# Graph layers on one core: edge keys made earlier, two groups of them compared in the first product unit, and the third adjacency load put behind the first three loads of H rows

## What is computed

```
msgs = x[src]
out = x @ root + bias
for r in range(8):
    mask = (edge_type == r)
    sums = segment_sum(msgs * mask, dst)
    cnt  = segment_sum(mask, dst)
    out  = out + (sums / max(cnt, 1)) @ weight[r]
u = out
z = concat([u, x]) @ w_gate + b_gate
h = tanh(u) * z + x * (1 - z)
```

## Time and profile before

| What | us |
|---|---|
| runs of the kernel | 1172.08, 1175.61, 1187.93 |
| span of the profiled execution | 1185.5 |
| TensorE busy | 1102.5 (93%) |
| VectorE busy | 702.4 (59%) |
| ScalarE busy | 386.1 (33%) |
| GpSimd busy | 386.3 (33%) |
| end of the units on TensorE | 524.9 |
| first spread | 527.8 to 537.5 |
| second spread begins | 548.7 |

### The profile page before, as it was taken

One profiled execution on the slowest core, in us unless ns is written; L12 is line 12 of the kernel. 1 busy time (PEld: TensorE's weight loads), 2 busy tenths in 40 slices (PEclk: granted clock), 3 DMA queues, 4 the chain that ended last, 5 costly groups with the idle time before them and its releaser, 6 DMA issues.

```text
span 1185.5 us, 14272 instructions
## 1 busy us (share of the span) xinstructions
PE 1102.5 (93%) x5481; PEld 916.7 (77%) x5481; DVE 702.4 (59%) x1369; ACT 386.1 (33%) x598; POOL 386.3 (33%) x268
## 2 busy tenths in 40 slices
PE   5999999999999999986999998999979897989896
PEld 4778888888888888876999998887747675777774
DVE  7486666566666532105667766475587556656557
ACT  3222222222223332222332333441443324146652
POOL 6036655646565466623232230000100002410015
PEclk8999999999999999998999998999989898989997
DMA  8956678877567575457556442632330202576857
GB/s 324 416 184 143 143 208 202 204 221 160 143 142 147 129 169 125 75 155 225 173 168 207 114 119 74 209 142 77 55 85 38 71 2 73 192 233 231 271 171 248
DMA packets 84612, 191.77 MB, mean 162 GB/s; under 512 B 29080, under 2 KB 45275, under 8 KB 76089
## 3 DMA queue, kind: packets, MB, share of 16 engines
q1 hardware_dynamic: 36362, 123.40, 32.8%
q0 software_dynamic: 31968, 35.38, 14.1%
q10 hardware_dynamic: 16206, 32.00, 9.2%
HBM read 136.60 MB, written 54.15 MB: 161 GB/s over the span
## 4 chain that ended last, share of the span: by engine, by line
PE 70%; DMA 10%; DVE 10%; POOL 5%; issue 3%; ACT 2%; POOLq 0%; SPq 0%; DVEq 0%
PE ps L483 60%; POOL adj_scratch L1833 5%; DMA stage<-in_w_e 4%; DMA adj_scratch<-cnt,idx 3%; DVE rl L340 3%; PE ps L724 2%; PE ps L761 2%; DVE EQ L1236 1%; DMA stage<-h_scratch 1%; PE ps L690 1%; ACT rh L330 1%; PE ps L473 1%; PE ps L772 1%; PE ps L707 1%; DMA stage<-in_w_rel 1%
## 5 line engine op out<-in xcount | busy, mean ns | idle before, releaser
L340 DVE TENSOR_TENSOR rl<-stage,rh 128x512 fp32r<-128x512 f32 (+1 forms) x282 | 224.4, 826 | 336.4 <-ACT rh L330 316.5
L330 ACT CAST rh<-stage 128x512 fp32r<-128x512 f32 (+1 forms) x288 | 193.8, 709 | 530.9 <-PE ps L483 282.6
L1833 POOL DMA_INDIRECT adj_scratch<-cnt,idx x162 | 260.2, 1606 | 221.6 <-DMA adj_scratch<-cnt,idx 88.5
L483 PE MATMUL ps<-rh,xTh 128*125 128x512 f32 x800 | 316.5, 396 | 2.5 <-DVE U L1304 1.5
L483 PE MATMUL ps<-rl,xTh 128*125 128x512 f32 x800 | 315.0, 394 | 0.0
L483 PE MATMUL ps<-rh,xTl 128*125 128x512 f32 x800 | 314.6, 393 | 0.0
L483 PE MATMUL ps<-rh,Ar 125*125 125x342 f32 x600 | 193.3, 327 | 19.0 <-DVE rl L340 11.2
L483 PE MATMUL ps<-rl,Ar 125*125 125x342 f32 x600 | 192.3, 325 | 0.0
L483 PEld LDWEIGHTS ps<-rh,xTh 128*125 128x125 f32 x800 | 148.4, 185 | 40.3 <-DVE U L1304 2.0
L483 PEld LDWEIGHTS ps<-rh,xTl 128*125 128x125 f32 x800 | 148.7, 186 | 37.2
L483 PEld LDWEIGHTS ps<-rl,xTh 128*125 128x125 f32 x800 | 148.6, 186 | 36.0
(11 more groups left out here) (263 smaller groups left out, 1222.8 us busy)
## 6 DMA issues: line engine op xcount, KB each, us to landing
stage<-in_w_rel SPq DMA_DIRECT2D x32, 1024.0 KB
stage<-h_scratch SPq DMA_DIRECT2D x24, 855.0 KB
stage<-in_w_e SPq DMA_DIRECT2D x16, 1024.0 KB
adj_scratch<-Z POOLq DMA_DIRECT2D x16, 767.0 KB, 22.9
KR<-key_scratch ACTq DMA_DIRECT2D x27, 384.0 KB
h_scratch<-He ACTq DMA_DIRECT2D x40, 257.0 KB, 9.8
h_scratch<-He ACTq DMA_DIRECT2D x40, 256.0 KB, 9.1
stage<-in_w_gate SPq DMA_DIRECT2D x8, 1024.0 KB
```

The costliest lines, as they stand in the source:

```text
L330: e.copy(h, s).then_inc(*a_hi.up(*[("hi", t) for t in step(i)]))
L340: e.tensor_tensor(l, s, h.bitcast(F32), ALU.subtract).then_inc(*own.up(*[("lo", t) for t in step(i)]))
L483: ins = e.matmul(ps[0:P, b, 0:width], a, m, start=first and n == 0, stop=last and n == len(parts) - 1)
L1833: e.indirect_dma_start(accd, bass.IndirectOffsetOnAxis(ap=idx[:, n:n + 1], axis=0), cnt[:, n:n + 1], None, compute_op=ALU.add).then_inc(*d ...
```

## The change

Five edits:

1. DVE makes the keys directly behind the low parts of the first eight tiles, before chunk 2 of x is measured. ACT writes them to memory before the square root of chunk 2 (`root("n1", 2)`), and reads the first four groups back before it casts the turned chunk 3. TensorE transposes the keys behind chunk 0 and no longer behind chunk 1, and DVE copies them after chunk 3 is normalised, which is before chunk 3 is turned.
2. TensorE turns chunk c + 1, not c + 2, in the middle of chunk c, for c = 1 to 3: one chunk later than before.
3. DVE compares two groups of keys (EARLY = 2) in the first half of unit 0: group 0 before it evicts chunk 3, group 1 before chunk 4. All later groups move forward by two places, one half of a unit. ACT issues the rows of groups 4, 5 and 6 together at the first place.
4. SP loads the third adjacency (r = 2) behind the third load of H rows. The others keep their place behind the first load of their r.
5. The gate's bias (`BB`) is loaded late, behind the router's weights, and no longer at the start.

```diff
--- before.py
+++ after.py
@@ -39,6 +39,7 @@
 SW = 2048
 NHE = 8
 NB = 8
+EARLY = 2
 WINDOWS = (1, 5)
 ROWS = [[(slice(0, 128), c * P, 128)] for c in range(C - 1)] + [[(slice(0, 112), 500, 112), (slice(112, P), 612, 13)]]
 HALF = (slice(0, 512), slice(512, D))
@@ -405,7 +406,6 @@
             rows_in(U128, 4, d_x[4], ("x", 4))
             on.wait_ge(*at("x", 3))
             e.dma_start(BA128[:], rbias.partition_broadcast(128)).then_inc(*d_ba.up(("rbias",)))
-            e.dma_start(BB128[:], gbias.partition_broadcast(128)).then_inc(*d_bb.up(("gbias",)))
 
             def adjacency_in(r):
                 on.wait_ge(*at("adj", r - 2))
@@ -419,12 +419,13 @@
             for r in range(R):
                 for q in range(3):
                     load(first("h", r, q, 0))
-                    if q == 0 and 2 <= r + 2 < R:
+                    if q == (2 if r == 0 else 0) and 2 <= r + 2 < R:
                         adjacency_in(r + 2)
             for g in range(first("gate", 0, 0), first("gate", 0, 0) + 2):
                 load(g)
             e.dma_start(rw[:].rearrange("p k n -> p (k n)"), router).then_inc(*d_sm.up())
             e.dma_start(b1s[:].rearrange("p k n -> p (k n)"), b1).then_inc(*d_sm.up(("small",)))
+            e.dma_start(BB128[:], gbias.partition_broadcast(128)).then_inc(*d_bb.up(("gbias",)))
             for c in range(C):
                 on.wait_ge(*at("spread", R - 1, 2, C - 1))
                 rows_in(X128, c, d_xc[c], ("x again", c))
@@ -526,7 +527,7 @@
             turn("n1", 1, U, ("n1", "norm", 1))
 
             def keys_turned(c):
-                if c == 1:
+                if c == 0:
                     b, freed = banks.take(("keys",), ("key columns",))
                     for g in range(2):
                         on.wait_ge(*at("key rows"))
@@ -542,7 +543,7 @@
                     first = unit_tile(unit, hf, 0)
                     if unit == 0 and hf == 0:
                         by_chunk(("unit", 0, 0), first, 8, x_stat, freed, lambda c: (("n1", "lo", c, 1),), keys_turned,
-                                 lambda c: turn("n1", c + 2, U, ("n1", "norm", c + 2)) if c + 2 < C else None)
+                                 lambda c: turn("n1", c + 1, U, ("n1", "norm", c + 1)) if 1 <= c < C - 1 else None)
                         end_chunks(("unit", 0, 0))
                     else:
                         by_tile(("unit", unit, hf), first, 8, x_stat, freed)
@@ -970,24 +971,27 @@
             turned("n1", 0, xTh)
             turned("n1", 1, xTh)
             highs(8)
+            on.wait_ge(*at("key rows"))
+            e.dma_start(keyd.rearrange("(g p) q -> p g q", g=2), kr1[:]).then_inc(*d_key.up(("keys out",)))
             for c in range(2, C):
                 root("n1", c)
                 if c == 3:
-                    on.wait_ge(*at("key rows"))
-                    e.dma_start(keyd.rearrange("(g p) q -> p g q", g=2), kr1[:]).then_inc(*d_key.up(("keys out",)))
+                    for g in range(4):
+                        key_rows(g)
                 turned("n1", c, xTh)
             highs(10)
-            for g in range(4):
-                key_rows(g)
             g, s = 0, 0
             for unit in range(R + 1):
                 for hf in range(2):
                     if unit or hf:
                         for k in range(8):
                             highs(unit_tile(unit, hf, k) + RT)
-                            if k % 8 in WINDOWS and g < NG:
-                                if g + 4 < NG:
-                                    key_rows(g + 4)
+                            if k % 8 in WINDOWS and g < NG - EARLY:
+                                if g == 0:
+                                    for early in range(EARLY):
+                                        key_rows(4 + early)
+                                if g + EARLY + 4 < NG:
+                                    key_rows(g + EARLY + 4)
                                 g += 1
                     if unit == R and hf == 1:
                         adjacency_copy(0)
@@ -1255,6 +1259,12 @@
             lows(4)
             turned("n1", 1, xTh, xTl)
             lows(8)
+            on.wait_ge(*at("edges"))
+            e.scalar_tensor_tensor(out=kr0[:], in0=er[0][0:HR], scalar=float(RI), in1=er[1][0:HR], op0=ALU.mult, op1=ALU.add).then_inc(
+                *v_row.up(("key place",)))
+            on.wait_ge(*at("key place"))
+            e.scalar_tensor_tensor(out=kr1[:], in0=er[2][0:HR], scalar=float(N), in1=kr0[:], op0=ALU.mult, op1=ALU.add).then_inc(
+                *v_row.up(("key sum",)))
             measured(2)
             normed(2)
             for c in range(2, C):
@@ -1264,13 +1274,6 @@
                 if c + 1 < C:
                     normed(c + 1)
                 if c == 2:
-                    on.wait_ge(*at("edges"))
-                    e.scalar_tensor_tensor(out=kr0[:], in0=er[0][0:HR], scalar=float(RI), in1=er[1][0:HR], op0=ALU.mult, op1=ALU.add).then_inc(
-                        *v_row.up(("key place",)))
-                    on.wait_ge(*at("key place"))
-                    e.scalar_tensor_tensor(out=kr1[:], in0=er[2][0:HR], scalar=float(N), in1=kr0[:], op0=ALU.mult, op1=ALU.add).then_inc(
-                        *v_row.up(("key sum",)))
-                if c == 3:
                     on.wait_ge(*at("keys turned"))
                     e.tensor_copy(kc[:], ps[:, banks.of["keys",], 0:TILES]).then_inc(*v_out.up(("key columns",)))
                     on.wait_ge(*at("key columns"))
@@ -1297,6 +1300,9 @@
                                 g += 1
                     for c in range(C):
                         b = banks.of["unit", unit, hf, c]
+                        if unit == 0 and hf == 0 and c >= C - EARLY:
+                            key_window(g)
+                            g += 1
                         if unit == 0:
                             on.wait_ge(*at("unit", 0, hf, c))
                             on.wait_ge(*at("rbias"))
```

## The result

| | before | changed |
|---|---|---|
| median of 20 runs | 1182.18 | 1184.52 |
| lowest to highest | 1169.95 to 1194.42 | 1179.60 to 1190.13 |
| span of the profiled execution | 1185.5 | 1185.8 |

What follows compares the result with a forecast made beforehand. TensorE, busy 93% of the span, bounds the kernel, so only its waits can be won: 1185.5 - 16.5 (first spreads) + 9.2 (start) = 1178.2. Forecast 1179, own range 1175 to 1184, overall range 1166 to 1187.

Steps and rivals of the forecast that it cites:

- The stall: TensorE's waits at the first two spreads, 2.98 and 11.19 us, from late adjacency additions; removal with clock effects: 16.5 off.
- the release: TensorE's release by a VectorE eviction after the early comparisons, at 82.95 before; forecast 91.7 to 92.6.
- wait at tile 10: TensorE stands about 4.3 us for tile 10's low part, which VectorE makes behind two early comparisons.
- So 0 to 0.3 us of wait stay: At the second spread: H rows ready 7.0 to 7.9 us after the units' end, first spread ending at 7.96.
- The sum: For the first two spreads: 2.98 + 11.19 + 1.67 + 1 - 0.3 = 16.5 us off, bounds 15.5 and 17.5.
- The clock term: Second spread began slowly after its wait; full clock there to win 1 us, bounds 0 and 1.7.
- Nothing: Loading the gate's bias late, around 725 with the queue idle to 744, was to change no time.
- The median run has little left to win: Without the stall the profiled execution gives 1171.1, fastest run 1172.08; the start's 9.2 us are paid in every run.
- the four that change the time: Rivals: start costs less (0.2), runs differ for another reason (0.17), start costs more (0.07), additions become the bound (0.04).
- the start costs more: Rival: weight load at 9 us and slower restart make the start cost 13 to 16, total 1183 to 1187; chance 0.07.
- The additions become bound: Rival: additions land late again amid second-half weight traffic; at 18.5 us a group, 37 late, 1216; chance 0.04.
- The early comparisons do nothing for the additions: Rival: zeroes land only at 67, so earlier indices don't help; counted inside the forecast, no chance of its own.

Runs made afterwards that it cites:

- experiment 2: Kernel before, without the additions of the last two of 27 groups of keys; 1175.56 us, ratio 0.9863 to the kernel before.
- experiment 5: Changed kernel with EARLY = 0, all comparisons at their old places; 1177.36 us, ratio 1.0014 to the kernel before.
- experiment 6: Changed kernel with GpSimd's step on the key rows ahead of its 16 zeroing transfers; 1178.36 us, ratio 1.0041 to the kernel before.
- experiment 3: Changed kernel with GpSimd's copy of adjacency 0 held until the second spread's low parts are made; 1185.18 us, ratio 0.9955 to the kernel before.
- experiment 1: Kernel before with only the third adjacency load moved behind three H loads; 1181.55 us, ratio 0.9885 to the kernel before.
- experiment 4: Changed kernel with GpSimd's copy and first addition held behind the second and third spreads' low parts; 1180.49 us, ratio 0.9893 to the kernel before.
- experiment 7: Changed kernel with the third adjacency load back behind the first H load; 1185.46 us, ratio 1.0077 to the kernel before.
- experiment 8: Kernel before with the later adjacency load, both GpSimd holds and the first comparison in VectorE's idle time; 1172.23 us, ratio 0.9963 to the kernel before.
- experiment 12: Changed kernel with EARLY = 1, key rows ahead of the zeroing transfers and both GpSimd holds; 1173.32 us, ratio 0.9874 to the kernel before.
- experiment 13: Changed kernel with the gate's bias loaded at the start again; 1180.82 us, ratio 1.0075 to the kernel before.
- experiment 14: Kernel of experiment 12 with the gate's bias loaded behind the branch, after the second load of x; 1174.41 us, ratio 1.0008 to the kernel before.
- experiment 10: Changed kernel run again, unaltered, beside the kernel before on chip C; 1184.23 us, ratio 1.0016 to the kernel before.
- experiment 11: Changed kernel with key rows before zeroing, EARLY = 0, one comparison in VectorE's idle time and both GpSimd holds; 1179.52 us, ratio 0.9969 to the kernel before.

## Why the prediction was right or wrong

**The bound** was read rightly. The stall hangs on the landings of 27 groups, a later end of the units absorbs it, and the runs' scatter is this stall (experiment 2, and the two spreads of 24.5 and 10.5 us).

**Edits 1 and 2: the mechanism right, the size a little short.** Key rows done at 26.98 (forecast 27.2), TensorE stands 7.1 for them. The 15 matmuls behind took 6.37, the forecast's upper end was 5.8, and the turn of chunk 4 ended at 47.8 (forecast 46.5 to 47.4). Without the early comparisons (experiment 5) the units end 1.5 later, not 2.6 to 3.5, because the 1.51 of wait at the release swallows most of the rest; in the changed kernel that is hidden by edit 3.

**Edit 3: right.** 4.27 of wait at tile 10 (forecast 4.3), release at 92.77 (forecast 91.7 to 92.6), 9.8 on against 9.2, units' end 534.56 (533 to 535). Experiments 5 and 6 show that it needs the late key rows and the early comparisons together.

**Edit 4: the mechanism right where it applies, one term wrong.** "So 0 to 0.3 us of wait stay" is the step that failed: 3.40 stayed. The sum took "1.94 to 2.83, rows of 1.94 being the usual ones" for the low parts and didn't ask what made the 2.83 one. The earlier trace rows show it only when this row of GpSimd, in the kernel before, is put beside it:

```profile
544.03 2.78 POOL L1844 COPY Atot<-Ar 128x3125 f32<-128x3125 f32 x1 [25.38 <-DMA h_scratch<-He]
```

The copy ran to 546.81, and the low part that started at 545.77 ended at 548.60. The end of a held low part is 1.79 to 1.81 behind the end of GpSimd's instruction in these five cases: before (548.60, 546.81), changed (545.97, 544.17), experiment 2 (537.60, 535.79), experiment 3 (552.97, 551.18), and experiment 1 (555.65, 553.85). When the stall went, the low part moved to the copy's start, and so was held for nearly all of it. In all sixteen profiles 123 low parts of H rows start inside a GpSimd copy or addition of this sum, and all end 1.78 to 1.82 behind it; the 245 that no such instruction touches take 1.92 to 1.94. Not all of VectorE's work is held: 469 evictions into U, which read one operand from `ps`, start inside the same instructions and take their usual 0.57 to 0.58. Experiments 3 and 4 show it by taking it away. The Trainium skill ("SBUF — State Buffer", section "Who interferes with whom") says that a VectorE instruction with two SBUF inputs contends with a GpSimd one that reads SBUF, and its section on the two sides says that the one that starts first keeps the shared ports for the whole instruction. The trace agrees: the held instruction needs 1.80 after the release, about the low part's own 1.94.

The size comes out too. A low part that starts 0.08 after the copy (541.46, 541.38) ends at 541.38 + 2.79 + 1.80 = 545.97, which is 2.57 later than 541.46 + 1.94; with the 0.83 that stay when nothing holds it (experiments 3 and 4) that is the 3.40.

The sum also took 16.5 off for edit 4 and 9.2 on for the start as if each came by itself. In the changed kernel the stall goes without edit 4: experiment 7 has the old place of the load and waits 3.35. It is the start, by ending the units late and the additions early, that takes the 11 us away, and edit 4 is shown to work only in experiment 1. That the sum came as near as it did is luck in this respect.

**The clock term.** The 1 us taken for a slow second spread wasn't won, because the first matmul behind the wait of 3.40 is as slow as behind that of 11.19 (0.65 in both). The term itself was there: from the start of the second spread to TensorE's stop at the branch it is 177.87 before and 177.85 in the changed kernel, and 176.48 in experiments 4, 8 and 12, which wait 0.83 and start it with 0.42. So it is worth 1.4, inside the bounds of 0 to 1.7.

**Edit 5 "Nothing": wrong by 1.3 us.** The cover named, SyncE's idle queue up to 744, was there; what was overlooked is that TensorE stands at a branch 1 us later. Experiments 13 and 14 show the wait to follow the transfer. That instructions behind the branch are fetched by transfers that queue with it is the reading that fits (the profile lists "instruction" queues among the DMA's), and wasn't tested on its own. The other 1.6 of the 2.93 lie behind the branch and are scatter as far as can be told: from there to the end the sixteen profiles take 451.24 to 455.82, the kernel before 454.16, the changed one 455.82 and, in its second profile (experiment 10), 452.65.

**"The median run has little left to win"** led to about the right size for a wrong reason. The sum of 1178.2 is a span; the runs list a time 1.7 above the span, so it stands for 1180, and for an execution like the one profiled, not for the median. The forecast for the median rested on three runs, one at 1187.93. On chip A the kernel before has 16 us to win (experiment 2), on D next to nothing. The changed kernel's time hardly knows of that, 1184.52 and 1184.23: its sign against the kernel before is a matter of where the additions land. Per group of six the profiled executions show 15.9 to 16.9 us.

**The rivals.** None of the four that change the time came true in the changed kernel. The median, 1184.52, falls by its number into the range of "the start costs more" (1183 to 1187), but the start cost 9.7 and not 13 to 16. "The additions become bound" did in experiment 11. "The early comparisons do nothing for the additions" held in its reason: the indices stood at 58.78, the first addition went out at 62.20, and in experiments 3 and 6, where it went out at 61.90 and 62.15, the profile names the zeroing as its releaser. They did gain 9.3 us for the additions, which weren't needed, since the units had become 9.7 late.

**Open:** what makes landings late on one chip and not on another; the release wait of 5.69 in kernel 12; the one run of 2791.86 in experiment 5; the gain of 1.2 us at the branch, in runs.

## What to carry to other kernels

Before a stall is taken out, put every engine's row beside the work that will follow it: the instruction that was due in the shadow of the stall now meets whatever else was waiting for the same event, here GpSimd's copy. A row that is longer than its like has a cause, and the sum needs it before it takes "the usual one". And a kernel whose time hangs on a chain of landings has no single time before: one early comparison that made the units end 0.4 or 2.8 us later (experiments 8 and 12) did better than two that cost 9.7.

## What the runs showed of the hardware

- A VectorE subtraction of two SBUF tiles (1.94 us alone) that starts inside a GpSimd copy, or addition, ends 1.78 to 1.82 us after it, 123 times of 123 in sixteen profiles. A VectorE eviction that adds a product from `ps` into U takes its usual 0.57 to 0.58 us beside the same instructions.
- TensorE's stop at a branch, 4.68 to 4.85 us, became 5.91 to 6.59 with a 512 KB transfer sent out 1 us before it.
- The same program with 162 chained indirect additions has a median of 1173 us on one chip and of 1190 to 1193 on another, twice; the kernels of experiments 14 and 12, in which the additions have more lead, have medians of 1174.41 and 1173.32 on the same two chips.
